# An attention and mixture-of-experts layer on one core: the second batch's norm statistics move to ScalarE, its projections to the front and its rotation to GpSimd, the causal masks are added in row halves, and the order is written anew

## The reference

```python
q = rope(xn @ wq); k = rope(xn @ wk); v = xn @ wv        # 16 query heads, 4 key/value heads of 16 numbers
attn = softmax(where(causal, q @ k.T / 4, -inf))         # 4 query heads share one key/value head
attention = (attn @ v) @ wo
scores = xn @ router_w.T                                 # 8 experts, the best 2 of each token, softmax over the two
experts = sum over the two of weight * ((silu(xn @ w1[e]) * (xn @ w3[e])) @ w2[e])     # bfloat16, 64 hidden each
```

## Time and profile before

| | us |
|---|---|
| median of 3 runs | 308.0 (307.36 to 308.73) |
| the profiled execution | 307.04 |
| its span, first to last instruction | 305.1 |
| PE, DVE, ACT, POOL busy in the span | 273.7, 241.2, 225.6, 126.2 |

### The profile page before, as it was taken

The page is one execution under the profiler, slowest core; times in us unless marked ns, Lnnn a source line. Parts: engine busy times, 40 slices in busy tenths (PEclk is TensorE's granted clock), DMA queues, the critical chain, the costliest instruction groups (busy, mean ns, idle before and its releaser), DMA issues.

```text
span 305.1 us, 6697 instructions
## 1 busy us (share of the span) xinstructions
PE 273.7 (90%) x2234; PEld 111.3 (36%) x2243; DVE 241.2 (79%) x362; ACT 225.6 (74%) x450; POOL 126.2 (41%) x253
## 2 busy tenths in 40 slices
PE   0757578989999999999998999999999999999996
PEld 0434223333433243243432334346423364233245
DVE  2698987999899999998868898997698977632242
ACT  1143224789699889999889889974799778999950
POOL 7379461434746464240663273443302512312510
PEclk9999955999999999999999999999999999999999
DMA  7446416010001205201426800141120230310213
GB/s 247 132 91 117 87 38 121 20 22 17 4 0 23 52 12 112 52 4 18 88 52 107 226 21 2 36 37 34 20 70 2 52 54 2 98 26 2 66 41 103
DMA packets 49024, 17.60 MB, mean 58 GB/s; under 512 B 43104, under 2 KB 48480, under 8 KB 48992
## 3 DMA queue, kind: packets, MB, share of 16 engines
q1 hardware_dynamic: 48304, 16.39, 25.2%
q10 hardware_dynamic: 688, 0.79, 0.8%
HBM read 4.46 MB, written 2.10 MB: 22 GB/s over the span
## 4 chain that ended last, share of the span: by engine, by line
PE 74%; DVE 8%; ACT 5%; issue 4%; DMA 4%; POOL 2%; SPq 2%; ACTq 0%; DVEq 0%; POOLq 0%
PE ps L740 20%; PE ps L722 14%; PE ps L707 12%; PE ps L687 7%; DVE PM L597 6%; PE ps L700 5%; PE ps L780 5%; PE ps L759 4%; ACT PR L480 4%; PE ps L749 3%; PE ps L778 3%; DMA X<-x 2%; DMA STACKS<-MIXED 2%; PE ps L767 1%; PE ps L678 1%
## 5 line engine op out<-in xcount | busy, mean ns | idle before, releaser
L480 ACT ACTIVATE PR<-ps,SCALE 128x512 f32<-128x512 f32 (+1 forms) x320 | 184.6, 651 | 32.2 <-PE ps L722 29.6
L597 DVE TENSOR_REDUCE PM<-ps 128x8 f32<-128x1024 f32 x144 | 168.7, 1219 | 11.3 <-PE ps L707 10.0
L418 POOL TENSOR_SCALAR_AFFINE_SELECT PR<-PR 128x512 f32<-128x512 f32 x64 | 39.9, 637 | 96.6 <-ACT PR L480 96.6
L740 PE MATMUL ps<-PR,VA 128*32 128x512 f32 (+3 forms) x768 | 78.1, 496 | 0.1
L722 PE MATMUL ps<-STACKS 64*128 64x512 f16 (+3 forms) x384 | 73.9, 333 | 2.5 <-DMA STACKS<-MT 0.8
L707 PE MATMUL ps<-STACKS 64*128 64x128 f16 (+2 forms) x640 | 61.5, 274 | 7.2 <-DVE PM L597 5.7
L707 PEld LDWEIGHTS ps<-STACKS 64*128 64x128 f16 x640 | 24.2, 97 | 58.7 <-issue 55.2
L722 PEld LDWEIGHTS ps<-STACKS 64*128 64x128 f16 x384 | 23.9, 95 | 53.4 <-ACT PR L480 41.0
L740 PEld LDWEIGHTS ps<-PR,VA 128*32 128x32 f32 x768 | 16.9, 108 | 26.7 <-issue 20.6
L687 PE MATMUL ps<-WP,XT 128*128 128x392 f32 x64 | 25.0, 522 | 1.6 <-ACT XT L451 1.6
L433 POOL TENSOR_TENSOR HB<-MIXED,GATE 128x512 bf16<-128x512 f32 x16 | 16.5, 1044 | 18.9 <-DVE MIXED L650 17.3
(11 more groups left out here) (82 smaller groups left out, 219.7 us busy)
## 6 DMA issues: line engine op xcount, KB each, us to landing
X<-x SPq DMA_DIRECT2D x8, 256.0 KB, 6.3
out<-X SPq DMA_DIRECT2D x16, 128.0 KB, 1.8
MIXED<-w SPq DMA_DIRECT2D x3, 512.0 KB, 3.7
STACKS<-MT SPq DMA_DIRECT2D x64, 2.0 KB
WP<-w_proj ACTq DMA_DIRECT2D x1, 392.0 KB, 4.3
WO<-wo ACTq DMA_DIRECT2D x1, 256.0 KB, 6.0
STACKS<-MIXED SPq DMA_TRANSPOSE x16, 3.8
MT<-MPW SPq DMA_TRANSPOSE x16, 2.4
```

The lines of the kernel that those rows point to most:

```text
L418: mask = g.affine_select(out=blk, in_=blk, compare_op=ALU.is_ge, fill=0.0, base=0, pattern=[[0, GRP], [1, P]], channel_multiplier=-1)
L480: a.activation(PR[:, k % RING, j, 0:width], bank(step)[:, 0:width], ACT.Exp, scale=SCALE[:]).then_inc(s_exp, 1)
L597: v_.tensor_reduce(spots, two_banks(step).rearrange("p h (a s n) -> p h a s n", a=2, n=P), AX.X, ALU.max).then_inc(m_max, 1)
L740: mm = t_.matmul(o_bank[VW * j:VW * (j + 1), CHUNK - width:CHUNK], VA[:, b * KVH + grp, kb, :], PR[:, n % RING, j, at:at + width], start=i ...
```

## The change

- The moments of tiles 8 to 15 leave DVE: ACT takes them with two instructions a tile (`N`, each with an accumulated sum), and one step of POOL (`R`) makes all eight deviations. ACT norms tiles 4 to 15 (`z`), DVE only 0 to 3.
- ACT also writes `XNB`, straight from PSUM.
- The projections of tiles 8 to 15 are steps `J`. They use the banks of the scores. ACT copies their 320 columns to `PJ` in SBUF, with scores and values; so DVE takes no part. POOL rotates each tile from there with four instructions (`q`).
- The mask of a diagonal step is four matmuls of 64 rows and 256 columns instead of two of 128 and 512: `SHOW_TO[half]` times a 64x64 `HIDE`, for each half of the keys and each of the two banks, the two banks on different halves of the array. The tables are built by POOL on 64 partitions and copied to the others by one transfer.
- The largest weight is found by one reduction with absolute values, not three instructions.
- All five order strings are new.

```diff
-        "pxxPjjxxjjxxxjjxjjmmmmmmmmmmmmmmssmssmssmmssvmssxmssmssmsssmvmssmsvsmsmssvmsssmvsmssmvsssmsmvssmssms"
+        "xpxxPjjjxxxjxxjjjjmmmmmxxxmmJmJmmJmxmxxmJmJxmmJmsxmJmssmssmssmssmsvssmssmvssmsvmssmJmsmssvsmsssmvmss"
...
-    ("DVE", "z"): range(QT),
-    ("POOL", "z"): range(QT, TILES),
+    ("ACT", "z"): range(CQ, TILES),
...
+            sp.wait_ge(ruled, 7)
+            sp.dma_start(MASKS[ROWS:P], MASKS[0:ROWS]).then_inc(halved, 16)
...
+                elif kind == "deviations":
+                    pool.wait_ge(squares, QT)
+                    g.tensor_scalar(SQUARES[:], SQUARES[:], 1.0 / D, LN_EPS, ALU.mult, ALU.add).then_inc(ve2, 1)
+                    pool.wait_ge(ve2, 1)
+                    g.tensor_tensor(RSTD[:, QT:TILES], SQUARES[:], NHALF[:], ALU.pow).then_inc(spread, 1)
+                    pool.wait_ge(spread, 1)
+                    g.tensor_tensor(SHIFT[:, QT:TILES], LESS[:], RSTD[:, QT:TILES], ALU.mult).then_inc(shift2, 1)
+                elif kind == "rotated":
+                    pool.wait_ge(v_spread, n + 1)
...
+                    g.tensor_tensor(rc, pj, cos, ALU.mult)
+                    g.tensor_tensor(rr[:, :, 0:half], pj[:, :, half:HD], sin[:, :, 0:half], ALU.mult)
+                    g.tensor_tensor(rr[:, :, half:HD], pj[:, :, 0:half], sin[:, :, half:HD], ALU.mult).then_inc(crossed, 1)
+                    pool.wait_ge(crossed, n - QT + 1)
+                    g.tensor_tensor(QK[:, n % 2], RC[:, n % 2], RR[:, n % 2], ALU.add).then_inc(turned_on, 1)
...
-                    after(act, xb_sb, n - 1)
-                    a.copy(XT[:, n % 2], bank(step)[:, 0:D].rearrange("p (k n) -> p k n", k=KT)).then_inc(xt_sb, 1)
...
+                    turned = bank(step)[:, 0:D].rearrange("p (k n) -> p k n", k=KT)
+                    a.copy(XT[:, n % 2], turned).then_inc(xt_sb, 1)
+                    a.copy(XNB[:, :, n * P:(n + 1) * P], turned).then_inc(xb_sb, 1)
+                elif kind == "spread":
+                    act.wait_ge(x_in[(QT + n) // 2], 16)
+
+                    after(act, squares, n)
+                    a.activation(SPARE[:], X[:, QT + n, :], ACT.Copy, scale=-1.0 / D, accum_out=LESS[:, n:n + 1]).then_inc(less, 1)
+                    act.wait_ge(less, n + 1)
+                    a.activation(SPARE[:], X[:, QT + n, :], ACT.Square, bias=LESS[:, n:n + 1], accum_out=SQUARES[:, n:n + 1]
+                                 ).then_inc(squares, 1)
...
+                        act.wait_ge(pk_ps, n + 1)
+                        a.copy(PJ[:, n], bank(step)[:, 0:QK_COLS])
...
-                        if diagonal:
-                            hide = HIDE[:].unsqueeze(1).broadcast_to([P, CQ, P])
-                            t_.matmul(bank(step, h), IDB[:], hide, start=True, stop=False, skip_group_check=True)
+                    if diagonal:
+                        if n == 0:
+                            pe.wait_ge(halved, 16)
+                        for half in range(2):
+                            for h in range(PILE):
+                                rows = slice(ROWS * h, ROWS * (h + 1))
+                                keys = bank(step, h).rearrange("p (s a k) -> p s a k", s=CQ, a=2)[:, :, half, :]
+                                t_.matmul(keys, SHOW_TO[half][rows], HIDE[rows].unsqueeze(1).broadcast_to([ROWS, CQ, ROWS]),
+                                          start=half == 0, stop=False, skip_group_check=True)
```

More of the change, by code:

```diff
@@ L135 @@
 )
-KINDS = dict(W="largest", p="range", P="scales", n="moments", z="norm", x="turned", j="project", l="parts", k="stacks", m="maxima", M="rows",
+KINDS = dict(W="largest", p="range", P="scales", n="moments", N="spread", R="deviations", z="norm", x="turned", j="project", J="projected", q="rotated", l="parts", k="stacks", m="maxima", M="rows",
              t="rows_turned", u="rows_placed", s="scores", v="product", r="untwisted", b="quotients", g="rank", G="weigh", c="cast", e="experts",
@@ L198, in build @@
         IDF = sb("IDF", [P, P])
-        IDB = sb("IDB", [P, P], BF16)
-        HIDE = sb("HIDE", [P, P], BF16)
+        MASKS = sb("MASKS", [P, ROWS + 2 * P], BF16)
+        HIDE = MASKS[:, 0:ROWS]
+        SHOW_TO = [MASKS[:, ROWS + a * P:ROWS + (a + 1) * P] for a in range(2)]
         ONE = sb("ONE", [1, P])
@@ L345, in _ @@
             g.memset(IDF[:], 0.0).then_inc(zeroed, 1)
[L346 to L347 removed]
+            g.memset(MASKS[:], 0.0).then_inc(zeroed, 1)
             g.memset(MPW[:], 0.0).then_inc(zeroed, 1)
             g.memset(NHALF[:], -0.5).then_inc(zeroed, 1)
[L350 to L354, removed]
[L355 removed]
+            pool.wait_ge(zeroed, 4)
+            g.affine_select(out=IDF[:], in_=IDF[:], compare_op=ALU.not_equal, fill=1.0, base=0,
+                            pattern=[[-1, P]], channel_multiplier=1).then_inc(made, 1)
+            upper, last = slice(0, ROWS), ROWS - 2
+            for t, op, first, fill in ((HIDE, ALU.is_ge, 0, -BIG), (SHOW_TO[0], ALU.not_equal, 0, 1.0),
+                                       (SHOW_TO[1], ALU.not_equal, ROWS, 1.0)):
+                g.affine_select(out=t[upper], in_=t[upper], compare_op=op, fill=fill, base=first,
+                                pattern=[[-1, t.shape[1]]], channel_multiplier=1).then_inc(ruled, 1)
+            pool.wait_ge(ruled, 3)
+            for t, fill in ((HIDE, -BIG), (SHOW_TO[0], 0.0), (SHOW_TO[1][:, 0:ROWS], 1.0), (SHOW_TO[1][:, ROWS:P], 0.0)):
+                g.affine_select(out=t[upper], in_=t[upper], compare_op=ALU.is_ge, fill=fill, base=last,
+                                pattern=[[0, t.shape[1]]], channel_multiplier=-1).then_inc(ruled, 1)
             g.memset(ONE[:], 1.0).then_inc(made, 1)
@@ new lines, in _ @@
+                    turned = bank(step)[:, 0:D].rearrange("p (k n) -> p k n", k=KT)
[8 more added lines that the diff above has]
+                                 ).then_inc(squares, 1)
+                elif kind == "norm":
+                    if n < QT:
+                        act.wait_ge(shift, (n - CQ) // 2 + 1)
+                    else:
+                        act.wait_ge(shift2, 1)
+                    after(act, xt_ps, n - 3)
+                    a.activation(XN[:, n % 4], X[:, n, :], ACT.Identity, bias=SHIFT[:, n:n + 1], scale=RSTD[:, n:n + 1]
+                                 ).then_inc(xn[1], 1)
+                elif kind in ("project", "projected"):
+                    if kind == "project":
+                        act.wait_ge(rot, n + 1)
+                        b, taken = 0, v_taken
+                    else:
+                        act.wait_ge(pk_ps, n + 1)
+                        a.copy(PJ[:, n], bank(step)[:, 0:QK_COLS])
+                        b, taken = 1, v_spread
+                    a.copy(RS[:, b * QT + n, :], bank(step)[:, R_COL:PROJ])
+                    a.copy(VA[:, b * KVH:(b + 1) * KVH, n, 0:HD],
+                           bank(step)[:, V_COL:R_COL].rearrange("p (g d) -> p g d", g=KVH)).then_inc(taken, 1)
```

135 lines of the change are left out of this document (72 added, 63 removed).

## The result

The changed kernel takes 291.1 us (median of four runs, 289.94 to 292.22) where the kernel before takes 308.4 beside it (four runs, 307.36 to 309.85). The ratio is 0.944, with a 95% interval of 0.938 to 0.949: 5.6% faster. Forecast were 292.5 us.

The account below looks back on a forecast made before the run. PE was taken to bound from 60 to 290.4 us, DVE the front. Span 305.1 + 0.5 (front) - 12.0 (projections) - 6.5 (masks) + 1.0 (tail) + 2.0 (coupling) = 290.1; as measured time 292.5 us, range 284 to 303.

Parts of the forecast that it names:

- Masks: Diagonal steps: PE time falls from 0.54 to 0.22 us at best; 22 steps after 60 us save 6.5 us.
- Projections of batch 1: Seven projections and seven transposes leave PE's stretch after 60 us, at 1.41 + 0.30 each: 12.0 us saved.
- coupling: After 60 us: near-full engines wait for each other more, adding 2 us to PE's 7.2 us of waits.
- DVE's lost rotation: After 60 us: DVE loses eight rotations, 8.9 us in all, by itself free, so nothing in the sum.
- Front: Up to the 15th score: projections fit under DVE's maxima; the point comes at 60.5 us, 0.5 later than before.
- It is DVE that sets both: In the front: DVE sets when the 15th score comes in the old order (60) and the new (60.5 us).
- ACT's front: Before the first exponential: ACT's added moments, norms and copies at 0.40 us an instruction are covered; at 0.69 not.
- Rival 2: Until the first score: ACT is too full, the front comes 5 to 8 us later, 297.5 to 300.5; chance 0.11.
- rival 3: In the front: the clock stays low until the first score, 13.7 us later, 306, no change; chance 0.05 in full.
- rival 4: POOL's rotations ahead of triangles delay the products and stop PE: 16.5 to 21 us, 309 to 313.5; chance 0.06.
- Tail: Behind the last product: the last `E` stands there and adds 1.0 us.
- ACT and not PE full in the middle: Sign of being wrong: the middle would show ACT full, where PE was forecast at 96% or more.

Follow-up runs that it names:

- b_front6: Kernel before with six idle projections added among its first 14 maxima, the eight real ones of batch 1 left in the middle: 311.37 us (ratio 1.011).
- a_poolless: Changed kernel with the three multiplies of each of POOL's rotations over one head of 20 instead of all: 290.9 us (ratio 0.942).
- a_jlate: Changed kernel with norms, transposes and projections of tiles 12 to 15 moved from the front to between scores 17 and 67: 306.03 us (ratio 0.990).
- a_dverot: Changed kernel with DVE instead of POOL doing batch 1's three rotation multiplies a tile, POOL keeping the addition: 302.76 us (ratio 0.979).

## Why the prediction was right, and which step was not

- *Masks.* Forecast 0.54 to 0.22 at best; measured 0.21 and 0.23, so the lower price was right. Undone they cost 6.8, forecast 6.5, but the agreement is luck: 4.4 of it are in the middle, where all of the 6.5 were to be, and 2.8 in the front, which was to have nothing. A step undone in the middle costs 0.20 us and not the 0.32 of its PE work. By the rule cited from the Trainium skill (TensorEngine Tiling (Array Packing), Key Properties) the sum would have had 7.0; the run cannot tell 6.5 from 7.0.
- *Projections of batch 1.* Forecast 12.0 for seven tiles with transposes, which is 1.41 for a projection and 0.30 for its transposes; put back as bare PE work, projections cost 1.3 each. The transposes alone were not tested.
- *The whole middle.* Projections, masks and coupling were to give 16.5; it gave 20.5. The 2.0 for coupling did not come: PE's idle time was 7.2 us in 60 to 290.4 and is 7.7 in 60 to 274. Without that term the sum gives 18.5. But the masks measured 4.4 and seven projections 9.5, together 13.9. The other 6.6 are the transposes, DVE's lost rotation and the new order, which the sum had at 2.1, at nothing and at nothing.
- *Front.* Forecast 0.5 us late at the 15th exponential, measured 3.4. The first mask was right (29.7 for 30.0), the first exponential came at 53.0 for 51.5. "It is DVE that sets both" failed: from 34.5 to 52 PE is full, DVE waits for PE four times (0.33 to 0.84 us each) and ACT waits for it too (2.08, 1.49 and 0.62 us before a copy). PE was to have 17.1 us of work up to the first score; it is busy for 19.9 from 29.7 to 52.0, part of it at half clock. With DVE's maxima halved the front ends no earlier (63.9). In ScalarE's and VectorE's timelines two of these waits read

```profile
39.48 0.37 ACT L489 COPY XT<-ps 128x256 f32<-128x256 f32 x1 [2.08 <-PE ps L749]
...
49.70 2.36 DVE L657 TENSOR_REDUCE PM<-ps 128x8 f32<-128x1024 f32 x2 [0.84 <-PE ps L775]
```

  The rest comes behind the first score: the seventh `J` stands there (53.00; not behind the second, as said above), and PE's string has 25 maxima ahead of the 15th score, not about 24.
- *ACT's front.* The accumulating activations were priced at 0.40, and ScalarE's timeline shows each followed by a read of the accumulator:

```profile
25.44 0.47 ACT L495 ACTIVATE SPARE<-X 128x256 f32<-128x256 f32 x1
25.76 0.24 ACT L495 ACTIVATION_READ_ACCUMULATOR SPARE<-X 128x1 f32 x1
26.03 0.51 ACT L497 ACTIVATE SPARE<-X,LESS 128x256 f32<-128x256 f32 x1
26.45 0.19 ACT L497 ACTIVATION_READ_ACCUMULATOR SPARE<-X,LESS 128x1 f32 x1
26.54 0.35 ACT L489 COPY XT<-ps 128x256 f32<-128x256 f32 x1
```

  A tile's moments hold ACT for 1.10 us (25.44 to 26.54), not 0.80: 2.4 us more over eight tiles, and the norms had a mean duration of 0.60 for 0.40. That did not decide here, since the moments are done at 31.4 and PE comes to the transposes behind them only at 34.5. Rival 2 did not come true.
- *Clock.* It is low from 34.3 to 37.8, after 4.3 us in which PE worked 1.93 and waited for DVE 0.71 to 0.76 us at a time, and it came back with PE full. b_front6 shows the same: rival 3 fell. The Trainium skill (TensorE: Matmul & The Clock Gate, HAM oscillation) has the clock halved after the array waits for data; here the waits were for banks that DVE had to free, and the clock fell to 0.50.
- *POOL.* Rotation forecast 2.75 us a tile, measured 863 + 527 + 521 + 861 ns = 2.77; its price of nothing held (a_poolless, middle 211.7 in both), rival 4 fell. *Tail:* 1.0 forecast, 0.9 measured.
- *The step that failed* is in the reading of the kernel before: the middle was taken as one stage in which "PE bounds", with DVE's slack at 18%, and DVE's lost rotation as "by itself free". The same rows say otherwise when they are read one by one: DVE was at 19.25 of 20 and 71.71 of 80 up to 160 us; then at 86.37 of 100, and only after 260, at 11.30 of 30.40, is its slack large. Two runs show it: the new masks take some 7 us of PE work out of that middle and bring 1.8, and DVE's rotation put back costs 7.8 in the middle of the kernel after. As a pure relief DVE's work was indeed worth little: 60 us less of it bring 3.5 in the middle of the kernel before and 2.8 in that of the kernel after. And one of the prediction's own signs of being wrong, ACT and not PE full in the middle, holds from 80 to 160 us (77.85 against 76.46 of 80), though not over the whole of it.

So the total was right in part for a reason the prediction did not have. With DVE's multiplies back the middle is 219.4 us, 12.7 less than in the kernel before and not 20.5: part of the gain came only because DVE lost its 9 us there in the same step (at most these 7.8, since the multiplies put back were slowed beside POOL and waited for it once). Put back one at a time, the masks cost 6.8, eight projections 10.4 and DVE's rotation 11.6, together 28.8, where the whole change gave 17.3. Much of that excess lies in the front; in the middle they cost 4.4, 10.8 and 7.8, together 23.0 against 20.5. So there the additions nearly add up, and it is the reliefs that do not: 2.8 and 1.9 alone, 10.0 together. The two errors in the total, 2.9 too little for the front and 4.0 too little for the middle, had opposite signs and cancelled by luck.

Open remains what share of a_jlate's 14.9 the banks, ACT's work and the clock have, and how much of a_dverot's 11.6 would stay if POOL's work did not slow DVE. No run takes the new order, the copies of `XNB` on ACT or the norms off POOL by themselves, adds work to ACT alone, or relieves ACT in the kernel before; so that ACT bounded there too is not shown.

## What to carry to other kernels

Read an engine's cover in the stage where the work stands: DVE's 82% over the middle hid 91% in its first 100 us. Before work is called free, add it and also take something from the engine next behind, since in a balanced kernel adding can cost nearly the full price while relieving one engine gives little (2.7 us for 71 of DVE's); relieve two at once to see which bound stands behind. Split each run's difference by stage before it is compared with a term of the sum: the masks' 6.8 agreed with a forecast of 6.5 that had put it in another stage. Work that the bounding engine must do is best moved under another engine's bound, here the maxima of the kernel before, where a projection cost 0.5 us and not 1.3; the gain ends where that stage is full too, as the front of the kernel after is.

## What the runs showed of the hardware that was not expected

- An activation with an accumulated sum comes with a second instruction on ScalarE, 0.19 to 0.24 us each (16 of them, means 210 and 187 ns).
- DVE's multiply of two operands in SBUF took 0.32 us for 160 columns undisturbed and 0.75 to 0.98 beside working GpSimd, and 0.48 or 0.75 to 1.06 for 320; the reductions out of PSUM kept their 1.21. The Trainium skill (SBUF — State Buffer, Who interferes with whom) says that a DVE instruction with two SBUF inputs contends with a GpSimd instruction that reads SBUF; the trace agrees: all six slow multiplies overlap a GpSimd instruction that reads SBUF, none of the 18 others overlaps any.
- GpSimd's power took 1.65 us for 8 columns and 0.74 for 2.
